# Gated cross-attention and expert layer on one core: a table of routing steps, a later second chunk and idle matmuls for the first expert, the last wait on SyncE

## The reference, cut to what matters

```python
x = x + tanh(g_xattn) * attention(layernorm(x), ctx, ctx)
xt = layernorm(x).reshape(3584, 256)
S = sigmoid(xt @ Wg).T                          # 8 experts x 3584 scores
G, I = top_k(S, 896)                            # each expert takes its 896 best tokens
hid = gelu(xt[I] @ W1 + b1)                     # 896 x 1024 per expert
out = (hid @ W2 + b2) * G[..., None]
new_x = zeros.at[I.reshape(-1)].add(out)        # scattered back, added up
x = x + tanh(g_ffn) * new_x
```

## Time and profile before

| | |
|---|---|
| median of the runs | 944.60 us |
| the profiled execution's own time | 945.57 us |
| its span in the trace | 943.8 us |
| PE busy | 846.2 us, 90% |
| DVE busy | 694.2 us, 74% |
| ACT busy | 611.8 us, 65% |
| POOL busy | 235.8 us, 25% |

### The profile page before, as it was taken

How to read it: one execution, slowest core, us unless ns; L and a number is a source line. 1 busy time by engine, 2 the same in 40 slices (tenths; PEclk the granted TensorE clock), 3 DMA queues, 4 the chain that set the end, 5 groups by cost and what they waited for, 6 DMA issues and landing times. The chain is left out here.

```text
span 943.8 us, 22373 instructions
## 1 busy us (share of the span) xinstructions
PE 846.2 (90%) x8427; PEld 673.0 (71%) x8427; DVE 694.2 (74%) x1946; ACT 611.8 (65%) x1311; POOL 235.8 (25%) x202
## 2 busy tenths in 40 slices
PE   5898999999999999999998301899999999999994
PEld 3555777777777777777776100788888989888884
DVE  6786888888888888888885586678676767664541
ACT  2766787787787788788766111657494856757471
POOL 5650000000000000000000231166564756654403
PEclk9999999999999999999999555799999999999998
DMA  7836566566576566566511300334536152543203
GB/s 189 192 73 135 129 156 155 137 157 154 127 164 154 132 159 157 135 153 159 125 49 32 109 0 24 117 75 116 131 65 136 44 128 56 136 112 83 34 9 37
DMA packets 96211, 104.64 MB, mean 111 GB/s; under 512 B 11744, under 2 KB 92272, under 8 KB 96112
## 3 DMA queue, kind: packets, MB, share of 16 engines
q1 hardware_dynamic: 84128, 88.50, 37.1%
q0 software_dynamic: 10752, 14.69, 9.1%
q10 hardware_dynamic: 1232, 0.12, 0.1%
HBM read 39.60 MB, written 14.68 MB: 58 GB/s over the span
## 5 line engine op out<-in xcount | busy, mean ns | idle before, releaser
L430 DVE TENSOR_REDUCE a_nm<-a_pS 112x1 f32<-112x375 f32 x512 | 268.4, 543 | 53.6 <-PE a_pS L656 50.9
L286 ACT ACTIVATE a_P<-a_pT 128x448 f32<-128x448 f32 x258 | 135.6, 546 | 43.4 <-PE a_pT L650 43.0
L656 PE MATMUL a_pS<-a_kst,a_qst 96*112 96x375 bf16 x512 | 158.4, 330 | 3.2 <-DVE a_nm L430 2.9
L1527 PE MATMUL e_p<-w2hl,e_hh 128*128 128x512 f32 x448 | 159.7, 397 | 0.0
L650 PEld LDWEIGHTS a_pT<-a_qst,a_kst 98*128 98x128 bf16 x1536 | 105.9, 98 | 57.4 <-issue 13.4
L650 PE MATMUL a_pT<-a_qst,a_kst 98*128 98x112 bf16 x1536 | 139.1, 213 | 3.2 <-issue 1.6
L1529 PE MATMUL e_p<-w2hl,e_hl 128*128 128x256 f32 x448 | 125.1, 279 | 0.0
L294 ACT ACTIVATE a_kp<-a_pK,a_bk 128x375 bf16<-128x375 f32 x180 | 103.1, 573 | 28.4 <-PE a_pK L688 28.0
L1075 POOL MEMSET r_factors<- 128x1 f32 x15 | 0.6, 101 | 469.6 <-POOLq L62 469.4
L1357 POOL DMA_INDIRECT out_dram<-e_y,e_idx x56 | 89.4, 1596 | 110.0 <-ACT e_y L1386 102.2
L1430 DVE TENSOR_TENSOR e_hl<-e_hid,e_hh 128x384 fp32r<-128x384 f32 (+1 forms) x128 | 77.9, 623 | 51.0 <-ACT e_hh L1381 45.2
(11 more groups left out here) (217 smaller groups left out, 1528.6 us busy)
## 6 DMA issues: line engine op xcount, KB each, us to landing
a_kst<-a_kp SPq DMA_DIRECT2D x192, 192.0 KB, 3.6
w<-in_L_ffn_W_dram SPq DMA_DIRECT2D x16, 1024.0 KB
a_qst<-a_qp SPq DMA_DIRECT2D x96, 112.0 KB, 3.5
a_craw<-in_ctx_dram SPq DMA_DIRECT2D x32, 128.0 KB
a_room<-in_x_dram SPq DMA_DIRECT2D x8, 448.0 KB, 5.9
a_xb<-in_x_dram SPq DMA_DIRECT2D x32, 112.0 KB, 2.9
out_dram<-a_x SPq DMA_DIRECT2D x32, 112.0 KB, 1.9
xn_scratch<-a_x SPq DMA_DIRECT2D x32, 112.0 KB, 2.1
```

What stands on the lines that cost most here:

```text
L286: act.activation(P[(4 * b + quad) % 3][:, c, :], pT[u % 2][:, 0:4 * LQ], ACT.Exp).then_inc(exp_done, 1)
L430: dve.tensor_reduce(nm[:, h:h + 1], pS[h % 2][0:LQ, 0:LK], AXX, ALU.max, negate=True).then_inc(s_used, 1)
L656: pe.matmul(pS[h % 2][0:LQ, 0:LK], q_of(b, slice(0, ROWS), h), kst[b % 4][0:ROWS, h, 0:LK], start=True, stop=True).then_inc(s_ready, 1)
L1527: pe.matmul(p2[g % 2][:], hh[:, f, rows], T.w2hl[r % 2][:, f].rearrange("p q d -> p (q d)"), start=(f == 0), stop=(f == 7), skip_group_che ...
```

## The change

Four edits, all in the routing and in the experts' stage.

1. **A table of steps.** The steps of all eleven fine rounds, 0, 1, 2 and 3 times the round's unit, are made once (`steps`, 11 x 4 numbers in PSUM), from constants of POOL and the power of two that the coarse rounds found. The tries have a fourth column, the low end itself (`held_tries`), so that L1208 and L1217 go and `base` is one operation of four elements. The first operation, once, is 44 elements wide. POOL sets eight constants more and makes an iota and a product, ACT makes one copy more.
2. **The first expert's second chunk.** Its transposes, `tokens_high` and `tokens_low` leave step -1 and stand behind the first two of the sixteen blocks of step 0, on all three engines.
3. **Idle matmuls.** Before the wait for the gathered tokens PE gets 15 matmuls of 512 columns on weights that are there (`keep_clock`), and 6 more behind the first chunk's transposes. Their result is overwritten unread.
4. **The last wait** (`added`) is SP's instead of POOL's.

```diff
-            for r in range(ROUNDS - 4):
+            for r in range(FINE):
+                final = r == FINE - 1
                 counts()
-                if r > 0:
-                    n[0] += 1
-                    raised(r - 1, now).then_inc(v, 1)
-                    now = low[(r - 1) % 2][:]
-                if r < ROUNDS - 5:
-                    link(dve.tensor_scalar(gaps[(r + 1) % 3], gaps[r % 3], 0.25, None, ALU.mult))
-                    link(dve.tensor_scalar(base[:], gaps[(r + 1) % 3], now, None, ALU.add))
-                dve.wait_ge(v, n[0])
+                if not final:
+                    link(dve.tensor_scalar(base[:], steps[:, r + 1], held_tries[:, 0:1], None, ALU.add))
                 dve.wait_ge(summed, r + 5)
...
+            for r in range(FINE):
+                pool.memset(units[:, r], 2.0 ** (-3 - 2 * r)).then_inc(factors_set, 1)
...
+            pool.wait_ge(factors_set, 13 + FINE)
+            pool.tensor_tensor(spans[:], spans[:], units[:], ALU.mult).then_inc(factors_set, 1)
...
+            link(dve.tensor_scalar(steps, spans_in.rearrange("p (r j) -> p r j", j=4), power[:], None, ALU.mult))
+            link(dve.tensor_scalar(held_tries[:], steps[:, 0], now, None, ALU.add))
...
+            sp.wait_ge(added, NE * NG * 16)
...
-            pool.wait_ge(added, NE * NG * 16)
...
+                            if first and k == 1:
+                                tokens_high(1, 0)
...
+                            if first and k == 1:
+                                tokens_low(1, 0)
...
+                def keep_clock(n):
+                    for _ in range(n):
+                        pe.matmul(p1[2][:], T.w1h[0][:, 0, 0:128], T.w1h[0][:, 0, 0:512], start=True, stop=True)
+
...
+                            if first and 8 * c + f == 1:
+                                pe.wait_ge(gathered[1], 16 * 3)
+                                transposes(1, 0)
...
+                if not live(0):
+                    pe.wait_ge(T.w_high, 4)
+                    keep_clock(15)
                 if live(1):
                     pe.wait_ge(gathered[0], count(i, r, 1, 16 * 4, 16 * 4))
                     transposes(0)
+                if not live(0):
+                    keep_clock(6)
```

More of the change, by code:

```diff
@@ L1043, in routing @@
         pF = banks("pF", 1)[0]
[L1044 removed]
+        spans_in, steps = pF[:, 16:16 + 4 * FINE], pF[:, 64:64 + 4 * FINE].rearrange("p (r j) -> p r j", j=4)
+        base = sb("base", [128, 4])
         pT, pC, pP, pR = banks("pT", 1)[0], banks("pC", 1)[0], banks("pP", 1)[0], banks("pR", 1)[0]
@@ L1369, in step, with tokens_high @@
             def step(i, r, live):
+                first = isinstance(i, int) and i == 0 and r == 0
+                def tokens_high(c, off=1):
+                    g0, g1 = CHUNK[c]
+                    for kk in range(2):
+                        act.wait_ge(xt_ready, count(i, r, off, 4, 2 * c + kk + 1))
+                        act.activation(exh[:, kk, g0 * 128:g1 * 128], pT[kk][:, 0:(g1 - g0) * 128], ACT.Copy)\
+                           .then_inc(xh_done, 1)
                 if live(0):
@@ L1422, in at, with tokens_low @@
                     return count(i, r, 2, per, 0)
+                def tokens_low(c, off=1):
+                    g0, g1 = CHUNK[c]
+                    for kk in range(2):
+                        dve.wait_ge(xh_done, count(i, r, off, 4, 2 * c + kk + 1))
+                        dve.tensor_tensor(exl[:, kk, g0 * 128:g1 * 128], pT[kk][:, 0:(g1 - g0) * 128],
+                                          exh[:, kk, g0 * 128:g1 * 128].bitcast(F32), ALU.subtract).then_inc(xl_done, 1)
                 if live(0):
@@ L1449, in result @@
                     dve.tensor_tensor(y[g][:], p2[g % 2][:, D:2 * D], y[g][:], ALU.add).then_inc(y_read, 1)
[L1451 to L1455, removed]
-                                          exh[:, kk, g0 * 128:g1 * 128].bitcast(F32), ALU.subtract).then_inc(xl_done, 1)
                 if live(0):
@@ L1500, in step, with transposes @@
                 first = isinstance(i, int) and i == 0 and r == 0
+                def transposes(c, off=1):
+                    for kk in range(2):
+                        wait(pe, xl_done, count(i, r, off, 4, 2 * c + kk - 1))
+                        for g in range(*CHUNK[c]):
+                            last = pe.transpose(pT[kk][:, (g - CHUNK[c][0]) * 128:(g - CHUNK[c][0] + 1) * 128],
+                                                ex[:, g, kk * 128:(kk + 1) * 128], T.ident[:])
+                        last.then_inc(xt_ready, 1)
+                def keep_clock(n):
+                    for _ in range(n):
+                        pe.matmul(p1[2][:], T.w1h[0][:, 0, 0:128], T.w1h[0][:, 0, 0:512], start=True, stop=True)
                 if live(0):
@@ L1540, in step @@
                     second(2, 4)
-                def transposes(c):
-                    for kk in range(2):
-                        wait(pe, xl_done, count(i, r, 1, 4, 2 * c + kk - 1))
-                        for g in range(*CHUNK[c]):
-                            last = pe.transpose(pT[kk][:, (g - CHUNK[c][0]) * 128:(g - CHUNK[c][0] + 1) * 128],
-                                                ex[:, g, kk * 128:(kk + 1) * 128], T.ident[:])
-                        last.then_inc(xt_ready, 1)
+                if not live(0):
+                    pe.wait_ge(T.w_high, 4)
+                    keep_clock(15)
                 if live(1):
```

59 lines of the change are left out of this document (26 added, 33 removed).

## The result

The changed kernel takes 938.36 us (median of four, 937.30 to 939.44) against 944.59 before (four, 944.26 to 944.62), 6.2 us less; the ratio is 0.994, with an interval of 0.9927 to 0.9954. The forecast was 941.3, in a range of 939.5 to 943.0. The sign was right and about half of the gain was missed. The profiled execution took 937.30 us, with a span of 935.6.

What follows compares the result with a forecast made beforehand. PE is busiest, but the DVE–PE chain bounds routing, PE the experts' start, and 6.80 us at the end are idle. Rounds −1.85, experts −1.35, last wait −0.1 make −3.3: 944.6 to 941.3 us, range 939.5 to 943.0.

Steps and rivals of the forecast that it cites:

- Fine rounds: Routing: eleven rounds as long as the last one before, 22.22 us, 1.89 less; −1.85 with the table's cost.
- 44-wide operation: Routing: the one wider operation making the table costs about 0.04 us more than the one it replaces.
- POOL's and ACT's extra work: Routing: added constants, iota, product and copy, about 1.3 us, stay hidden in 3.1 us before PE needs them.
- Start of the experts: Experts' stage: idle matmuls raise PE's clock earlier and six transposes move behind two blocks; −1.35 us.
- the moved copies: First expert: ACT's 0.9 us and DVE's 1.1 us between the first blocks' activations cost nothing.
- The last wait: Kernel's end: moving the wait off POOL gives 0.1 us, within bounds of nothing to about 1 us.
- Sum: Whole kernel: −1.85 − 1.35 − 0.1 = −3.3 us, from 944.6 to 941.3 us.
- the first (939.7): Routing or end: rounds give −3.3 instead of −1.85, or the end gives 1 us; about 939.7, chance 0.17.
- The late clock: Start of experts: clock stays low until 594.2, the delay eats that gain; 942.7, chance 0.08.
- idle matmuls don't count: Start of experts: they fail to raise the clock, the kernel gets slower; 945.6 to over 946.5, chance 0.03.
- The stall: ACT's 1.77 us late in the experts goes with code place, may reach PE's path; 942.6 to 943.1, chance 0.10.
- The rule on transposes: Start of experts: PE transposes stay slow and don't raise the clock; all this part's gain gone, 942.6.

Runs made afterwards that it cites:

- tail_act: The kernel before with only the last wait moved from POOL to ACT; 944.01 us, ratio 0.9984.
- idle_only: The changed kernel with its idle matmuls, but the second chunk prepared ahead of the first block as before; 938.66 us, ratio 0.9941.
- tail_drain: The kernel before, last wait still on POOL, with a drain of POOL put ahead of that wait; 943.6 us, ratio 0.9986.
- the control: The kernel before, unchanged, run and traced once more; 944.45 us, ratio 0.9991.
- no_idle: The changed kernel without its 21 idle matmuls, second chunk still moved; 940.65 us, ratio 0.9959.
- experts_only: The kernel before with only the moved second chunk and the idle matmuls; 943.15 us, ratio 0.9973.
- after_again: The changed kernel, unchanged, run and traced once more; 938.41 us, ratio 0.9922.
- idle_first: The changed kernel with 12 idle matmuls directly behind the barrier and 8 behind the bias transpose; 937.61 us, ratio 0.992.
- idle_first_again: The changed kernel with 12 idle matmuls behind the barrier and 8 behind the bias transpose, measured once more; 939.46 us, ratio 0.9931.
- first_unmoved: The changed kernel with 12 idle matmuls behind the barrier, 8 behind the bias transpose, and the second chunk back in its place; 939.48 us, ratio 0.9934.

## Why the prediction was wrong, step by step

- *Fine rounds*: right. −1.89 was the working, −1.95 came; the last round of before was a good model of the new ones. The table's 44-wide operation took 0.27 us against 0.22, the expected 0.04. POOL's and ACT's extra work stayed hidden: from the routing's first operation to the first fine round it is 14.26 us against 14.23.
- *Start of the experts*: the mechanism was right, the size too small: −1.35 against −2.2, the mean of 14.70 of the three traces with this part against 16.90. The working had the transposes 9.32 us behind idx, and they came at 8.49 on average, 0.83 earlier. The way from there to the third block gave 0.25 more, and the mean of before, 0.23 below its first trace, takes that back. Two terms were mis-sized in those 9.32. I let the idle matmuls start 3.87 us behind idx (587.75 − 583.88), since the biases landed late in that one trace; in nine traces they landed 0.9 to 1.1 us earlier and only tail_act's did as late, and the idle matmuls started 2.80 us behind idx. And I took one number, 4.25 us, for the clock's rise. Behind the same 15 idle matmuls it was 3.5, 4.2, 5.9 and, in idle_only, 5.9 again; two of the four lie outside of the 3.67 to 4.86 that I allowed. From transposes to third block I had 6.46 us; 6.20 to 6.22 came. As I had expected, the moved copies cost PE nothing: from the third block to the second index copy 17.5 us passed, as before.
- *The last wait*: the step that failed. "I take 0.1, nearer to nothing, since POOL only leaves one wait and joins the same barrier" took POOL to lose no time between its wait and the barrier. It loses 1.6 us there, and tail_drain puts 1.3 of these down to POOL's drain. −1.6 us came, outside of the bounds of nothing to 1 us. The bounds were made from handovers between engines, and none of these rows has POOL behind a DMA that it issued. The figure of the Trainium skill that I set beside it ("Runtime: NRT & Kernel Launch", "The ~15µs preamble/postamble breakdown") left 1.8 us for the kernel, nearer to what came than my own bound, and I should have let it widen the range. With the wait on SP or ACT 5.3 us remain in the traces, close to its 5.
- *Sum*: −1.95 − 2.2 − 1.6 = −5.7 us against −3.3. Measured were −6.2, with an interval of 4.3 to 6.9 (0.9927 to 0.9954 of 944.6). The half microsecond between lies within that interval, and the attention alone scatters more. No errors cancelled: the rounds were sized right, and the other two terms were both too small.
- *Rivals*: the nearest was the first (939.7), and of its two reasons the end came, not the shorter rounds; for the end alone the working gives 940.4 (941.3 − 0.9), and 1.6 us came where it had 1. The late clock came in two traces (in the changed kernel it rose at 589.3, just before the idle matmuls ended, and in idle_only likewise) and still left a gain. That idle matmuls don't count is refuted: the clock rose during them in all seven traces that have them. The stall was real in the earlier trace rows, but none of the thirteen other traces showed it again, the control's among them; as far as they show it is not tied to the code's place. The rule that I set beside it, in the Trainium skill, "Runtime: NRT & Kernel Launch", "Instruction fetch mechanics", is for the target of a taken branch, and at 867 us ACT is in step 6, which the program has unrolled. The rule on transposes ("TensorE: Matmul & The Clock Gate", Part 4, in the Trainium skill) is not borne out: the eight transposes behind the idle matmuls took 1.03 us, against 1.94 in no_idle, where the clock was low. Whether transposes help to raise the clock, the other half of that rule, no run here tests.

What stays open is why the clock's rise takes 3.5 us in one execution and 5.9 in another, and why the clock falls once more in some executions of the attention.

## What to carry to other kernels

Here POOL issued the last DMAs and waited for them itself, and the end behind them was 1.6 us longer than with the wait on SP or ACT; where one engine does both at the end of a block, try the wait on another. Where PE stands idle ahead of a dense stretch, as here, fill the gap from its very start, not from the first convenient dependence, and end it when the data arrive: by the traces that gave another 0.5 to 1.4 us, though the totals can't show it. Before one trace's gap carries a term of the sum, ask whether it is a transfer's landing time, since that may be another one in the next execution. And before a difference of totals is explained, compare the granted clock of the stretches that the edit does not touch.

## What the runs showed of the hardware

With a drain of POOL ahead of its last wait the end behind the last DMA is about 1.3 us shorter (6.9 us against 5.56); with the wait on SP or ACT it is 5.3. PE's clock went from 0.50 to 1.00 between 2.9 and 5.9 us after the first idle matmul in the seven traces that have them (3.5 experts_only, 4.2 after_again, 5.9 changed and idle_only, 4.5 idle_first, 2.9 idle_first_again, 3.2 first_unmoved). In seven of fourteen traces of the same attention the clock fell to 0.50 at about 76 us for 3.4 or 6.8 us, and the attention ended 1.5 to 4.3 us later than in the others. The bias transpose, which waits for a load of 64 rows only, came 2.0 to 2.3 us behind the stage's first work in nine traces and 3.2 to 3.3 in two.
